# A four-layer graph network on one core: the second half's score preludes and the node-feature transfers move into the attention steps, and the output bias becomes a rank-one product

## What is computed

```
h = max(layernorm(x), 0)
x = x + layer(h)
```

```
h      = x @ W;  al_s, al_d = scores of h with a_src, a_dst
e      = leaky_relu(al_s[src] + al_d[dst])
alpha  = exp(e - max over dst) / (sum over dst)
out    = sum over edges of alpha * h[src], + bias
```

## Time and profile before

| | us |
|---|---|
| median of 3 runs (3750.87 to 3764.32) | 3754.76 |
| the profiled execution | 3760.77 |
| its span, first to last instruction | 3758.9 |
| PE busy | 3370.0 |
| DVE busy | 2365.7 |
| ACT busy | 840.5 |
| steps 0 to 7 and their end | about 1953 to 3273 |
| wide projection and `hmax` | about 3301 to 3423 |
| steps 8 and 9 | about 3439 to 3759 |

### The profile page before, as it was taken

The page is one execution under the profiler, slowest core; times in us unless marked ns, Lnnn a source line. Parts: engine busy times, 40 slices in busy tenths (PEclk is TensorE's granted clock), DMA queues, the critical chain, the costliest instruction groups (busy, mean ns, idle before and its releaser), DMA issues. The chain is left out here.

```text
span 3758.9 us, 33930 instructions
## 1 busy us (share of the span) xinstructions
PE 3370.0 (90%) x12562; PEld 1916.1 (51%) x12562; DVE 2365.7 (63%) x3107; ACT 840.5 (22%) x1110; POOL 664.4 (18%) x489
## 2 busy tenths in 40 slices
PE   6999857687999999999829999999999999985998
PEld 6897646564554554445414444444444444473444
DVE  9972212236011111434789989988998899858997
ACT  0113222235000000222202222222222222251222
POOL 2788888860000000000100000000000000010000
PEclk6559978898999999999959999999999999997999
DMA  9999968895434344222452222222222232385222
GB/s 346 365 285 248 264 168 222 236 259 123 142 126 132 124 138 139 88 78 64 143 175 67 62 67 88 87 70 87 75 76 74 81 96 72 108 253 166 66 66 67
DMA packets 255870, 525.90 MB, mean 140 GB/s; under 512 B 90569, under 2 KB 145631, under 8 KB 253407
## 3 DMA queue, kind: packets, MB, share of 16 engines
q1 hardware_dynamic: 139545, 432.89, 35.6%
q0 software_dynamic: 63680, 30.84, 5.8%
q10 hardware_dynamic: 52480, 60.01, 5.6%
HBM read 361.99 MB, written 161.67 MB: 139 GB/s over the span
## 5 line engine op out<-in xcount | busy, mean ns | idle before, releaser
L1141 PE MATMUL ps<-R,B 125*128 125x500 f32 x2800 | 1095.3, 542 | 20.1 <-DVE R L2030 12.7
L1141 PEld LDWEIGHTS ps<-R,B 125*128 125x128 f32 x2800 | 503.9, 190 | 591.5 <-issue 544.8
L695 POOL DMA_INDIRECT pairs<-w x400 | 620.4, 1551 | 201.9 <-issue 103.8
L991 PE MATMUL ps<-R,H 125*128 125x500 f32 (+1 forms) x1400 | 543.2, 543 | 15.1 <-ACT H L1225 7.6
L1352 ACT ACTIVATE R<-R,asc 125x1625 f32<-125x1625 f32 (+1 forms) x200 | 320.2, 1601 | 1020.8 <-DVE R L2017 1020.8
L2030 DVE SCALAR_TENSOR_TENSOR R<-R 125x1625 f32<-125x1625 f32 (+1 forms) x250 | 445.1, 1781 | 0.0
L2017 DVE SCALAR_TENSOR_TENSOR R<-H,asc 125x1625 f32<-125x1625 f32 (+1 forms) x200 | 369.0, 1846 | 114.1 <-PE ps L1148 87.3
L844 PE MATMUL ps<-R,H 125*128 125x375 f32 (+1 forms) x1000 | 303.2, 450 | 110.1 <-DMA R<-pairs 109.6
L991 PEld LDWEIGHTS ps<-R,H 125*128 125x128 f32 x1400 | 253.4, 191 | 284.0 <-issue 281.0
L1594 DVE TENSOR_TENSOR Fb<-Fb,ps 128x250 f32<-128x250 f32 (+1 forms) x140 | 67.2, 480 | 363.4 <-PE ps L844 305.6
L1141 PE MATMUL ps<-R,H 125*128 125x500 f32 (+1 forms) x700 | 276.5, 551 | 21.4 <-DVE R L2030 19.6
(11 more groups left out here) (309 smaller groups left out, 3036.9 us busy)
## 6 DMA issues: line engine op xcount, KB each, us to landing
pairs<-R SPq DMA_DIRECT2D x25, 3200.0 KB, 28.5
R<-ct_d SPq DMA_DIRECT2D x162, 406.2 KB, 3.2
R<-pairs SPq DMA_DIRECT2D x25, 2500.0 KB, 9.0
R<-ct_d SPq DMA_DIRECT2D x162, 375.0 KB, 3.1
R<-wt_d SPq DMA_DIRECT2D x50, 812.5 KB, 4.4
R<-wt_d SPq DMA_DIRECT2D x50, 750.0 KB, 4.2
wt_d<-R ACTq DMA_DIRECT2D x13, 1250.0 KB, 6.5
wt_d<-B ACTq DMA_DIRECT2D x12, 1250.0 KB
```

Source lines behind the costliest of these rows:

```text
L695: pool.indirect_dma_start(pairs, bass.IndirectOffsetOnAxis(ap=key_u[:, c:c + 1], axis=0), val[:, c, :], None, compute_op=ALU.add)\
L991: last = mm(ps[:, bank, at:at + w], rows[0:Q, j, f * 128:(f + 1) * 128], TL[q % TS][0:Q, o:o + w], start=j == 0 and at == 0, stop=j == NB ...
L1141: last = mm(ps[:, bank, at:at + w], rows[0:Q, j, f * 128:(f + 1) * 128], TT[q % TR][0:Q, o:o + w], start=j == 0 and at == 0, stop=j == NB ...
```

## The change

Four edits go together.

1. The prelude of the second half (three groups of columns, then the rows) leaves the place ahead of step 0 and ahead of step 8 and is done in pieces beside the units of that step: PE after units 1 to 4, DVE after units 3 to 6. SP stores and fetches its rows at unit 13 of the step instead of at unit 5 (step 0) or ahead of the step (step 8).
2. The store of the node features moves from SP's list ahead of the `LATE` loads to unit 13 of step 0. The readers of `X` that overwrite it wait for it later.
3. The read back moves from ahead of step 8 (right behind the last wide chunk) to unit 13 of step 8.
4. The bias add in step 8 is removed; each block of the wide projection gets one more product instead, a row of ones by the row `b32`. The denominator's places in steps 0, 2, 4 and 6 are swapped, so that step 0 does not write into `X`.

```diff
@@ -200,3 +200,3 @@
         denB = wB[:, CT * NYC * 6:CT * NYC * 6 + COLS[1]]
-        den_of = [denB if k % 2 else (PT[:, 0:LW] if k % 4 else Xf[:, 2 * LW:3 * LW]) for k in range(STEPS)]\
+        den_of = [denB if k % 2 else (Xf[:, 2 * LW:3 * LW] if k % 4 else PT[:, 0:LW]) for k in range(STEPS)]\
             + [PT[:, 0:LW], denB]
@@ -568,5 +568,2 @@
                 lc_load(r, *LATE[r])
-            sp.wait_ge(S("ln_done"), 4 * NB)
-            for p0, p1 in PART:
-                sp.dma_start(x_d[p0:p1, :], Xf[p0:p1, :]).then_inc(S("x_out"), 16)
             for r in range(LCR, len(LATE)):
@@ -584,4 +581,7 @@
                 lc_load(len(LATE) + q, j, k % 2)
-                if q == LCR - 1:
+                if q == LCR + 7:
                     uv_rows(1, 0, 1, 0)
+                    sp.wait_ge(S("ln_done"), 4 * NB)
+                    for p0, p1 in PART:
+                        sp.dma_start(x_d[p0:p1, :], Xf[p0:p1, :]).then_inc(S("x_out"), 16)
                 if j >= LCR and k >= 1:
@@ -612,4 +612,2 @@
                 wide_load(c)
-            for p0, p1 in PART:
-                sp.dma_start(Xf[p0:p1, :], x_d[p0:p1, :]).then_inc(S("x_back"), 16)
             sp.wait_ge(S("hmax"), 2 * NB)
@@ -619,3 +617,2 @@
             uv_rows(STEPS, HEADS, 0, 1)
-            uv_rows(STEPS + 1, HEADS, 1, 1)
             for q in range(STEPS * NB + LCR, (STEPS + 2) * NB):
@@ -624,2 +621,6 @@
                 lc_load(len(LATE) + q, j, k % 2)
+                if q == STEPS * NB + LCR + 7:
+                    uv_rows(STEPS + 1, HEADS, 1, 1)
+                    for p0, p1 in PART:
+                        sp.dma_start(Xf[p0:p1, :], x_d[p0:p1, :]).then_inc(S("x_back"), 16)
             out_v = out.rearrange("(j p) f -> p j f", p=Q)
@@ -1061,14 +1062,22 @@
 
-            def prelude(a0, sem, n0):
+            def prelude_first(a0, sem, n, n0, acc):
+
+                for g in range(len(MGROUPS[0])):
+                    bank = aux_bank(a0 + g, True, g == 0)
+                    if g == 0:
+                        pe.wait_ge(S(sem), n)
+                    max_columns(0, g, bank, acc)
+                uv_columns(n0, 0, aux_bank(a0 + PRE[0] - 1, True, False))
 
-                a = a0
-                for half in range(2):
-                    for g in range(len(MGROUPS[half])):
-                        bank = aux_bank(a, True, a == a0)
-                        if g == 0:
-                            pe.wait_ge(S(sem), len(EARLY) + len(LATE) // 2 * (half + 1) if sem == "l3_max" else 2 * NB)
-                        max_columns(half, g, bank, macc0 if sem == "l3_max" else macc)
-                        a += 1
-                    uv_columns(n0 + half, half, aux_bank(a, True, False))
-                    a += 1
+            def prelude_second(a0, sem, n, n0, acc, i):
+
+                if not 0 <= i < PRE[1]:
+                    return
+                bank = aux_bank(a0 + PRE[0] + i, False, False)
+                if i == 0:
+                    pe.wait_ge(S(sem), n)
+                if i < PRE[1] - 1:
+                    max_columns(1, i, bank, acc)
+                else:
+                    uv_columns(n0 + 1, 1, bank)
 
@@ -1139,3 +1148,3 @@
                         if j == 0 and bank == 6 and f == 0:
-                            pe.wait_ge(S("aux_free"), sum(PRE) if k == 0 else aux0[k - 1] if k < STEPS else aux0[k])
+                            pe.wait_ge(S("aux_free"), PRE[0] if k == 0 else aux0[k - 1] if k < STEPS else pre2 + PRE[0])
                         last = mm(ps[:, bank, at:at + w], rows[0:Q, j, f * 128:(f + 1) * 128], TT[q % TR][0:Q, o:o + w],
@@ -1152,6 +1161,8 @@
 
-            prelude(0, "l3_max", 0)
+            prelude_first(0, "l3_max", len(EARLY) + len(LATE) // 2, 0, macc0)
             for q in range(STEPS * NB):
                 unit(q, Bn)
-                if q >= NB:
+                if q < NB:
+                    prelude_second(0, "l3_max", 2 * NB, 0, macc0, q - 1)
+                else:
                     result(q // NB - 1, q % NB - 2)
@@ -1172,3 +1183,4 @@
                         last = mm(ps[0:Q, n % 4, 0:D + 2], slot[:, t, b * Q:(b + 1) * Q], w32[:, t, :],
-                                  start=t == 0, stop=t == CT - 1)
+                                  start=t == 0, stop=False)
+                    last = mm(ps[0:Q, n % 4, 0:D], ones[0:1, 0:Q], bcs[0:1, 4, :], start=False, stop=True)
                     last.then_inc(S("ring_pe"), 1)
@@ -1198,6 +1210,8 @@
 
-            prelude(pre2, "hmax", STEPS)
+            prelude_first(pre2, "hmax", 2 * NB, STEPS, macc)
             for q in range(STEPS * NB, (STEPS + 2) * NB):
                 unit(q, H)
-                if q >= (STEPS + 1) * NB:
+                if q < (STEPS + 1) * NB:
+                    prelude_second(pre2, "hmax", 2 * NB, STEPS, macc, q - STEPS * NB - 1)
+                else:
                     out_result(STEPS, q % NB - 2)
@@ -1356,2 +1370,4 @@
                 act.wait_ge(S("l3_pe"), (k + 1) * NB)
+                if k == 0:
+                    act.wait_ge(S("x_out"), 32)
                 if 1 <= k < STEPS:
@@ -1924,7 +1940,13 @@
 
-            def prelude_half(a, n, half, adc, hd):
-                for g in range(len(MGROUPS[half])):
-                    max_out(a + g, half, g, adc, hd, 6 + (a + g) % 2)
-                g = len(MGROUPS[half])
-                uv_out(a + g, n, half, 6 + (a + g) % 2)
+            def prelude_first_in(a, n, adc, hd):
+                for g in range(len(MGROUPS[0])):
+                    max_out(a + g, 0, g, adc, hd, 6 + (a + g) % 2)
+                g = len(MGROUPS[0])
+                uv_out(a + g, n, 0, 6 + (a + g) % 2)
+
+            def prelude_second_in(a, n, adc, hd, i):
+                if 0 <= i < PRE[1] - 1:
+                    max_out(a + PRE[0] + i, 1, i, adc, hd, 7)
+                elif i == PRE[1] - 1:
+                    uv_out(a + PRE[0] + i, n, 1, 7)
 
@@ -1997,3 +2019,3 @@
                 else:
-                    if q == 0:
+                    if k == 2:
                         dve.wait_ge(S("x_out"), 32)
@@ -2050,4 +2072,3 @@
                 if r == len(LATE) // 2 + 3:
-                    prelude_half(0, 0, 0, ad_of(0, 0), 0)
-            prelude_half(PRE[0], 1, 1, ad_of(0, 1), 0)
+                    prelude_first_in(0, 0, ad_of(0, 0), 0)
             def results_in(q):
@@ -2056,2 +2077,4 @@
                     result_in(k - 1, j - 2 - LATER)
+                else:
+                    prelude_second_in(0, 1, ad_of(0, 1), 0, j - 1 - LATER)
 
@@ -2090,4 +2113,3 @@
             link(ts(asb[0:Q, 2, :], ald[0:Q, :, 0], 0.2, None, ALU.mult))
-            prelude_half(pre2, STEPS, 0, ad_of(1, 0), HEADS)
-            prelude_half(pre2 + PRE[0], STEPS + 1, 1, ad_of(1, 1), HEADS)
+            prelude_first_in(pre2, STEPS, ad_of(1, 0), HEADS)
 
@@ -2116,6 +2138,7 @@
                 k, j = divmod(q, NB)
-                if k == STEPS and j == 8:
-                    dve.wait_ge(S("x_back"), 32)
-                    link(tt(X[0:Q, :, :], X[0:Q, :, :], bcs[0:Q, 4, :].unsqueeze(1).to_broadcast([Q, NB, D]), ALU.add))
+                if k == STEPS:
+                    prelude_second_in(pre2, STEPS + 1, ad_of(1, 1), HEADS, j - 1 - LATER)
                 if k == STEPS + 1:
+                    if j == 0:
+                        dve.wait_ge(S("x_back"), 32)
                     out_in(STEPS, j - 2 - LATER)
```

## The result

The changed kernel takes 3741.92 us (median of 9 runs, 3738.43 to 3744.38), the kernel before 3760.2 in the same comparison (9 runs, 3750.87 to 3768.24). The ratio is 0.9949, with a 95% interval of 0.9938 to 0.9961. The time fell by 18.3 us where I had forecast 29.9, and 3741.92 lies 0.9 above the top of my range. Part of that is the base: I counted from a median of 3754.76, and the kernel before has 3760.2 here, 5.4 more. The fall itself, 18.3, is inside the range's 14 to 44; the likeliest case's own range (22 to 38) it misses. The profiled span fell from 3758.9 to 3741.1.

The account below looks back on a forecast made before the run. PE was busy 90% of the span, but DVE or transfers came last where the change acts. Terms -7.5 - 3.2 + 2.9 - 9.6 - 12.5 = -29.9 us took the median 3754.76 to 3725, range 3711 to 3741.

Parts of the forecast that it names:

- the likeliest case: The main case, all parts summed: 29.9 us faster, reaching from 3717 to 3733 us; chance 0.65.
- Bias product: Wide projection: each of 25 one-row products costs a full row's 0.44 us, 10.9 us more on PE.
- the PE chain of my sum: End of `hmax` by PE: last block's evacuation at 3404.7, 0.7 us for it, then two `hmax` units, giving 3409.0.
- Store: Node features' store moved out of `EARLY`: removes two DVE waits for count loads, 7.5 us off; bounds 0 and 7.5.
- Second prelude, step 0: Ahead of step 0: 6.1 us leave the path, 2.9 come back inside the step, net -3.2.
- Second prelude, step 8: Ahead of step 8: hidden behind the rows' way through memory, so gains 0 and costs 2.9 inside the step.
- Bias add: Step 8: removing DVE's add saves 9.6 us, the 6.82 us instruction and the clock behind it; lower bound 6.
- Read back: Moved out of `hmax`: stage ends at 3410 instead of 3422.5, 12.5 us off; bounds 0 and 17.5.
- rival A: `hmax` gets no shorter since wide chunks alone delay POOL's loads; 12.5 us lost, -17.4 in all; chance 0.13.
- Transfers in their new places: Unit 13 of steps 0 and 8: cost 0, upper bound 4.5 us and about 3 more for a fallen clock.
- B: Steps 0 and 8: node features starve count loads on SP's queue, DVE stops, clock falls; -15 to -22; chance 0.07.
- C: Steps 0 and 8: B's mechanism far larger, kernel slower than before by 19 us and more; chance 0.03.

## Why the prediction was wrong, point by point

**Bias product, the step that failed.** I wrote that its price lay between 0 and the row's 0.44 us, and took the 0.44. The upper end was false. The product costs 0.80 us, 25 x 0.80 = 20.0 in place of 10.9, because it also pays for the change into it and out of it, 0.39 us a block. That is 9.1 us more on the PE chain of my sum, and the stage missed its forecast by 9.0. The closeness of the two numbers is in part luck. The sum took the later end of two chains, 3409.0 on PE and 3409.3 on DVE, and one us for count loads. On before's clock of events the stage ended at 3419.1, by PE's chain: 10.1 later than that chain's 3409.0, of which the product explains 9.1. The last us is mostly the block behind PE's gap, which ran at a lower clock (5.17 us for its 16 records against 3.75), and it took the place of the one for count loads, which did not come. The run over 128 rows closes the argument from the other side: with 0.41 us for the product the stage ends where the sum had it. The product's size was the term that was off, not the mechanism. What I had quoted from the Trainium skill ("TensorE: Matmul & The Clock Gate", "Why this matters for your kernels"), that a small contraction takes as long as a full one, holds for a run of such products (0.43 us for the second) and not for a single one between full ones.

**Store.** Right. Forecast 7.5, and the run that undoes it gives back 8.4 in the medians and 7.5 in the waits of its trace.

**Second prelude, step 0.** Right: `score` follows the last maximum directly, and the step takes 2.5 us more against 2.9. (The sum has 2.9 in each of the two steps. The last paragraph of the prediction says 2.9 for both together, which does not fit it; the sum was right.)

**Second prelude, step 8.** Right: 2.5 against 2.9, shown by the run that moves it back. It is a small loss at this place, hidden behind the others.

**Bias add.** Right by itself: step 8 is 7.3 shorter, 2.5 of prelude included, so 9.8 for the add against 9.6; the run that keeps the add measured 10.0. Undone by the product that replaced it.

**Read back.** The mechanism was right: the waits for counts went from 23.4 us to none. So rival A (the wide chunks alone hold POOL's loads back) is out, and the run without the product, where the waits stay at 3.4 us, shows it apart from the slower PE. The move's worth came to 8.0 in this kernel and 17.8 without the product; the latter is close to my upper bound of 17.5, which was worked out for a product that costs nothing.

**Transfers in their new places.** Right at 0; rivals B and C are out. The loads behind the features took up to 21.3 us, against the 34 + 3.2 that I had allowed at most, and the six units of lead covered them. The first one landed at 3503.7, behind the features' last packet (3501.9), as the forecast had it.

**Left over.** 2.3 us in step 9 and the end, of which 1.7 are PE's lower clock in step 9, told below; 0.5 between `hmax` and step 8, where SP issues the read of the rows 4.1 us after their store instead of 3.5; 1.0 ahead of step 0, where the kernels with the moved store have the same work up to this point and reach their first `weights` at 1943.3 to 1949.1, so that one us says nothing.

The time lies 0.9 above the range, and the base moved by 5.4 between the two measurements: from the base that I counted from, a fall of 18.3 gives 3736.5, inside it. So that it came out above the range is partly chance; that it missed the likeliest case is not. The range's fault was that it treated "no row of before shows so short a contraction" as a doubt below the nearest row only, so no case had the product dearer, though the text named that as what would make it wrong.

## What to carry to other kernels

When a vector add is replaced by one more product in a chain, price the change of shape on both sides of the product: a contraction of 1 or of 64 rows between full ones cost twice what a full one does here, and spreading it over 96 or 128 rows took the surplus away. Before work is handed to another engine, ask whether that engine is about to become the last one in the stage that gets it; here the product went into the stage that another edit had just freed. A large transfer that delays small ones on another queue may be harmless in the same stage once it is halved, cut up and paced; which of the three it takes was not tried. When the profile puts an engine's idle time down to "issue", look at what the program makes it wait for and at the granted clock of that engine.

## What the runs showed of the hardware

A product of 1 or 64 rows between products of 128 cost 0.19 us at each change, 0.39 for both, on top of its own 0.41, and one of 96 rows nothing. A product of 128 rows is half as dear there as one of a single row (0.41 against 0.80).

In step 9, behind `weights` of unit 4, DVE stands idle, and the profile puts it down to "issue". The row in three kernels: before, changed, and the one with step 8's prelude ahead.

```profile
3624.56 1.78 DVE L2017 SCALAR_TENSOR_TENSOR R<-B,asb 125x1500 f32<-125x1500 f32 x1 [4.42 <-issue]
```
```profile
3606.17 1.78 DVE L2039 SCALAR_TENSOR_TENSOR R<-B,asb 125x1500 f32<-125x1500 f32 x1 [6.11 <-issue]
```
```profile
3603.40 1.78 DVE L2039 SCALAR_TENSOR_TENSOR R<-B,asb 125x1500 f32<-125x1500 f32 x1 [2.73 <-issue]
```

In all thirteen kernels the idle time is 2.73 to 2.74, 4.42 to 4.44 or 6.11 to 6.12 us, and step 9 has 136.3, 138.0 or 139.7 with it. The cause is on PE. This is `score` of unit 7, and by the program it waits until PE has finished unit 3. PE's timeline of that unit's 12 records, in the same order:

```profile
3617.67 6.79 PE L1141 MATMUL ps<-R,H 125*128 125x500 f32 x12
```
```profile
3597.90 8.16 PE L1150 MATMUL ps<-R,H 125*128 125x500 f32 x12
```
```profile
3598.03 5.28 PE L1150 MATMUL ps<-R,H 125*128 125x500 f32 x12
```

In each of the thirteen `score` starts 0.1 us after they end. The stretch of the 12 records in the changed kernel and in the one with the prelude ahead (columns as in the earlier trace rows):

```profile
3597.90:3606.06 8.16, 8.16 (x15) 3.61 (x16) 2.16 (x3) 0.32 (x1) 0.00 (x0) 0.64 0.17 49
3598.03:3603.31 5.28, 5.28 (x16) 2.53 (x16) 2.64 (x3) 0.81 (x1) 0.00 (x0) 1.00 0.27 75
```

PE is busy in both, and its granted clock is 0.64 in the one, 0.77 in the kernel before and 1.00 in the other. In the changed kernel it is 0.50, the lower of the two levels (1.2 GHz), up to 3602.17. Ahead of these records PE did 13 products of a single column (26 records) for the denominator (L1090), which took 2.89 us where the clock was full and 3.38 in the changed kernel. The 2.88 us between the two rows of PE and these 0.49 make the 3.38 between the idle times. So 1.7 us of the forecast's miss are time at the lower clock. Why the clock falls there sooner in one kernel, later in another and in three not at all stays open.
